# First 160 edge tiles as one dense matrix in both graph convolutions

## What is computed

```python
def _gcn(x, W, b, src, dst, w, n):
    h = x @ W
    agg = segment_sum(w[:, None] * h[src], dst, num_segments=n)
    return agg + b

f1 = layernorm(x)                              # 6250 x 256
h  = _gcn(f1, W1, b1, ...)                     # first convolution
z  = leaky(concat([h, root row of f1]))
z  = leaky(_gcn(z, W2, b2, ...))               # second convolution
x  = x + leaky(concat([z, root row of h]) @ Wl + bl)
n  = layernorm(x)
weights = n @ wr + br                          # router: the 3124 rows with the largest weights are chosen
x  = x + n + (chosen rows: (gelu(n @ w1 + b1) @ w2 + b2) * weight)
```

## Time and profile before

| | us |
|---|---|
| time, median of 3 runs | 2068.99 (2068.99 to 2077.73) |
| span of the profiled execution | 2915.3 |
| PE busy in it | 1865.9 |
| DVE busy | 1169.0 |
| GpSimd busy | 1474.9 |
| ACT busy | 369.1 |
| mean granted share of TensorE's full clock | 0.808 |

### The profile page before, as it was taken

One profiled execution on the slowest core, in us unless ns is written; L12 is line 12 of the kernel. 1 busy time (PEld: TensorE's weight loads), 2 busy tenths in 40 slices (PEclk: granted clock), 3 DMA queues, 4 the chain that ended last, 5 costly groups with the idle time before them and its releaser, 6 DMA issues.

```text
span 2915.3 us, 49425 instructions
## 1 busy us (share of the span) xinstructions
PE 1865.9 (64%) x7011; PEld 1437.8 (49%) x7012; DVE 1169.0 (40%) x4136; ACT 369.1 (13%) x927; POOL 1474.9 (51%) x1571
## 2 busy tenths in 40 slices
PE   0465646655555556354637888886777686757687
PEld 0344535434443444333526666665666465645475
DVE  6543333332332332222324455444544434434356
ACT  4200000000000000000101111111111111111111
POOL 5455555554555554455344555555555554545430
PEclk9788778777776776767878889988988888978797
DMA  6422222222222322222432222222222222222212
GB/s 202 131 83 81 80 80 80 84 78 74 82 81 78 88 79 75 70 79 77 152 98 72 72 72 81 78 79 75 78 81 76 81 71 69 83 62 82 67 50 88
DMA packets 120873, 244.27 MB, mean 84 GB/s; under 512 B 32822, under 2 KB 71046, under 8 KB 120748
## 3 DMA queue, kind: packets, MB, share of 16 engines
q0 software_dynamic: 73664, 200.90, 24.0%
q1 hardware_dynamic: 35612, 32.02, 3.5%
q10 hardware_dynamic: 11472, 10.27, 1.1%
HBM read 223.42 MB, written 19.64 MB: 83 GB/s over the span
## 4 chain that ended last, share of the span: by engine, by line
SPq 53%; issue 35%; PE 5%; DVE 3%; DVEq 1%; another core or an unknown queue 1%; DMA 1%; ACT 1%; ACTq 0%
SPq L348 45%; SPq L343 7%; PE ps_agg L716 2%; PE ps_dn L854 1%; PE ps_up L865 1%; DVE fw2s L1062 1%; DVE S L1153 0%; ACT xs L480 0%; DVE ring L1442 0%; DMA normed_rows<-xs 0%; DVEq L1193 0%; PE ps_o L804 0%; DVE acc L1161 0%; PE ps_dn L852 0%
## 5 line engine op out<-in xcount | busy, mean ns | idle before, releaser
L716 PE MATMUL ps_agg<-ring,S 128*128 x3136 | 912.1, 440 | 677.0 <-SPq L355 320.3
L716 PEld LDWEIGHTS ps_agg<-ring,S 128*128 128x128 f32 x3136 | 669.1, 221 | 860.1 <-issue 757.8
L434 POOL DMA_INDIRECT ring<-conv_rows,idx x752 | 714.5, 950 | 632.4 <-DVEq L1188 424.2
L434 POOL DMA_INDIRECT ring<-normed_rows,idx x736 | 701.1, 953 | 631.7 <-DVEq L1188 426.7
L1153 DVE TENSOR_SCALAR S<-iota,dstc,wc 128x128 f32<-128x128 int16 x1584 | 454.9, 353 | 377.1 <-issue 360.3
L1161 DVE TENSOR_TENSOR acc<-acc,ps_agg x490 | 206.3, 421 | 893.4 <-PE ps_agg L716 478.4
L716 PE MATMUL ps_agg<-ring,S_more 128*128 x768 | 265.7, 506 | 254.6 <-DVE S_more L1153 150.0
L716 PEld LDWEIGHTS ps_agg<-ring,S_more 128*128 128x128 f32 x768 | 187.6, 254 | 321.3 <-issue 287.9
L854 PE MATMUL ps_dn<-fw2s,hT 128*128 128x256 f32 x848 | 232.7, 434 | 0.0
L854 PEld LDWEIGHTS ps_dn<-fw2s,hT 128*128 128x128 f32 x848 | 179.4, 218 | 49.5 <-issue 21.7
L865 PE MATMUL ps_up<-xnT,fw1s 128*128 128x256 f32 x800 | 195.0, 400 | 8.9 <-issue 7.1
(11 more groups left out here) (248 smaller groups left out, 1077.2 us busy)
## 6 DMA issues: line engine op xcount, KB each, us to landing
ring<-normed_rows SPq DMA_DIRECT2D x2048, 1.0 KB
ring<-conv_rows SPq DMA_DIRECT2D x2048, 1.0 KB
ring<-conv_rows,idx POOLq DMA_INDIRECT x752
ring<-normed_rows,idx POOLq DMA_INDIRECT x736
conv_rows<-rows ACTq DMA_DIRECT2D x49, 128.0 KB
xs<-in_x SPq DMA_DIRECT2D x6, 640.0 KB
out_rows<-xs SPq DMA_DIRECT2D x3, 1024.0 KB
xs<-in_x SPq DMA_DIRECT2D x2, 1280.0 KB
```

Of the source, the lines that this page charges most:

```text
L434: pool.indirect_dma_start(out=ring[:, slot * TG + t, :], out_offset=None, in_=rows_of, in_offset=bass.IndirectOffsetOnAxis(ap=at, axis=0)) ...
L716: last = nc.tensor.matmul(to, select[:, t, :], moving, start=(t == 0), stop=(t == TG - 1))
```

## The change

The first 160 tiles (`NM`), which hold all edges whose destination is in windows 0 and 1, are taken out of the rounds. They become one matrix A with 256 columns (the destinations) and 50 blocks of 128 rows (the source nodes), held in SBUF in the place of `xs`. A round now has 12 tiles (`QG = 3`), the ring holds six groups, and there are 52 rounds (`NIT = NW + 3`). Steps start in round `lag`, which is now at least 4. With these inputs it comes out as 6, so 46 rounds have a step and two steps are left for after the last round.

Building A takes rounds 1 to 40 of the first convolution, four tiles a round. For each tile DVE writes a one-hot matrix of `src mod 128` (128 columns) and one of a key that joins `dst` within 5 nodes and the source block (245 columns, times the weight), PE multiplies them, and DVE adds the 49x5 result into A at a column read from a table. Rounds 41 to 50 multiply A by the rows in 10 chunks of 5 blocks and add 128x512 to windows 0 and 1. A is also stored to HBM. In the second convolution each round starts with one block of A (128x256, loaded by SyncE with its block of `conv_rows`), two matmuls into one half of `ps_agg` and one add of 128x512. SyncE's single-row copies and their tables are gone, so GpSimd gathers all other tiles: 622 per convolution, 22 of them from the raw input.

A branch for inputs in which one of the first 160 tiles spans more than 5 nodes (`rare_edges`) is there too; here the widest spans 5 nodes, so it is not taken.

The core of the diff:

```diff
-    QG = 4
+    QG = 3
+    NIT = NW + 3
+    NM = NT - NIT * RING
+    MW = 2
+    SPAN = 5
+    KEYS = SPAN * NW
+    BPER = 4
+    B_IT = 1 + NM // BPER
+    CHUNK = 5
@@ sync
-                    for i in range(FAR_PASS):
-                        p = c * FAR_PASS + i
-                        sp.dma_start(ring[p:p + 1, SLOTS * TG + b, :].bitcast(i8), rows_of[ds(offsets[i], D * 4)].unsqueeze(0)).then_inc(far_landed[l][b], 16)
+            def load_block(i):
+                a = max(0, NW - 1 - i)
+                m = a + 1 if i < NW else 0
+                sp.dma_start(block_a, a_dram[:, m, :]).then_inc(block_loaded, 16)
+                sp.wait_ge(t2_stored, 16 * (NW - a + 2))
+                sp.dma_start(block_t, t2_dram[a * P:(a + 1) * P, :]).then_inc(block_loaded, 16)
...
+            for i in range(1, NIT):
+                sp.wait_ge(block_used, i)
+                load_block(i)
@@ tensor
+            def build_tiles(it):
+                pe.wait_ge(build_added, it * BPER + 1)
+                pe.wait_ge(build_ready, it)
+                for t in range(BPER):
+                    last = nc.tensor.matmul(up_banks[:, t // 2, t % 2 * KEYS:(t % 2 + 1) * KEYS], src_hot[:, t, :], key_hot[:, t, :], start=True, stop=True)
+                last.then_inc(build_done, 1)
...
+            def dense_block(it):
...
+                pe.wait_ge(block_loaded, it * 32 + 32)
+                pe.wait_ge(acc_step[1], i + 1)
+                for m in range(MW):
+                    to = flat(ps_agg[:, ds(i & 1, 1), m * D:(m + 1) * D])
+                    last = nc.tensor.matmul(to, block_a[:, m * P:(m + 1) * P], block_t, start=True, stop=True)
+                last.then_inc(mm_done[1], 1)
+            def edge_round(l, it, steps, s=None, matrix_work=True):
+                if l == 1:
+                    dense_block(it)
+                for q in range(QG):
+                    edge_group(l, it, q)
+                    if l == 0 and q == 1 and matrix_work:
+                        first_nodes(it)
+                    for piece in steps[q] if steps else ():
+                        piece(s)
-            rounds(1, (turn_step1, ffn_step_a, conv_step1, ffn_step_b), NW - 1, late_weights_in)
+            rounds(1, ((turn_step1,), (ffn_step_a,), (conv_step1, ffn_step_b)), NW - 1, late_weights_in)
@@ vector
+            def add_block(i):
+                dve.wait_ge(mm_done[1], i + 1)
+                dve.wait_ge(acc_step[1], i + 1)
+                dve.sem_inc(block_used, 1)
+                V.tensor_tensor(first_acc, first_acc, flat(ps_agg[:, ds((i + 1) & 1, 1), :]), op=ALU.add).then_inc(acc_step[1], 1)
+            def hot_tiles(it):
+                for t in range(BPER):
+                    at = within(dve.snap(it * BPER + (t - BPER)), NM - 1)
+                    V.tensor_scalar(src_hot[:, t, :], iota[:, 0:P], src_low[:, ds(at, 1)], None, ALU.is_equal)
+                    last = V.tensor_scalar(key_hot[:, t, :], iota[:, 0:KEYS], keys[:, ds(at, 1)], wc[:, ds(at, 1)], ALU.is_equal, ALU.mult)
+                last.then_inc(build_ready, 1)
+            def add_tiles(it):
...
+                    base = within(dve.value_load(base_row[0:1, ds(at, 1)]), MSPAN - SPAN)
+                    to = matrix[:, :, ds(base, SPAN)]
...
+                    dve.wait_ge(build_added, it * BPER + (t + 1))
+                    of = up_banks[:, t // 2, t % 2 * KEYS:(t % 2 + 1) * KEYS].rearrange("p (r a) -> p a r", a=NW)
+                    V.tensor_tensor(to, to, of, op=ALU.add).then_inc(build_added, 1)
@@ edge_round of vector
-                    select_ahead(l, it, q)
...
+                    if l == 1 and q == 0:
+                        add_last(l, p0 - 1)
...
                     dve.sem_inc(group_used[l], 1)
+                    select_ahead(l, it, q)
+                    if l == 1 and q == 0:
+                        add_block(p0)
...
-            rounds(1, (x1_step, norm_step, no_step, no_step), NW - 1, last_norm)
+            rounds(1, (x1_step, norm_step, no_step), NW - 1, last_norm, lambda: dve.wait_ge(x_again, 16 * (len(XCH) + len(PART))))
```

More of the change, by code:

```diff
@@ L352, in far_done @@
[L352 to L368 removed]
+            sp.dma_start(*big_loads[2]).then_inc(last_layer_loaded, 16)
@@ L513, in rounds @@
                 with act.Fori(0, stop) as s:
-                    for q in range(QG):
-                        steps[q](s)
+                    for piece in steps:
+                        piece(s)
             def stage_sums(l, s):
@@ new lines, in dense_chunk @@
+            def dense_chunk(it):
+                half = within(pe.snap((it + B_IT) & 1), 1)
+                to = up_banks[:, ds(half, 1), :].rearrange("p b n -> p (b n)")
+                f0 = within(pe.snap(half * CHUNK), CHUNK)
+                pe.wait_ge(chunk_copied, it + 1)
+                pe.wait_ge(dense_added, it + 1)
+                pe.wait_ge(chunk_loaded[0], ((it + 1) >> 1) * 16 + 1)
+                pe.wait_ge(chunk_loaded[1], (it >> 1) * 16 + 1)
+                for m in range(MW):
+                    for k in range(CHUNK):
+                        row = within(pe.snap(f0 + k), 2 * CHUNK - 1) if k else f0
+                        last = nc.tensor.matmul(to[:, m * D:(m + 1) * D], chunk_a[:, k, m * P:(m + 1) * P], flat(blocks[:, ds(row, 1), :]), start=(k == 0), stop=(k == CHUNK - 1))
+                last.then_inc(dense_done, 1)
@@ L748, in rounds @@
+            def rounds(l, steps, stop, ahead_of_steps):
                 pe.reg_mov(extras, 0)
                 pe.reg_mov(step, 0)
-                d = within(pe.snap(first), NIT, 1)
-                with pe.Fori(0, d) as it:
-                    for q in range(QG):
-                        edge_group(l, it, q)
-                if ahead_of_steps is not None:
-                    ahead_of_steps()
+                d = within(pe.snap(first), NIT, NIT - NW + 1)
+                if l == 0:
+                    with pe.Fori(0, 1) as it:
+                        edge_round(l, it, None, None, False)
+                with pe.Fori(1 - l, d) as it:
+                    edge_round(l, it, None)
+                ahead_of_steps()
@@ L765, in rounds @@
                     with pe.Fori(done, stop) as s:
-                        for q in range(QG):
-                            steps[q](s)
-            def no_step(s):
-                pass
+                        for group in steps:
+                            for piece in group:
+                                piece(s)
             def first_root_term():
@@ L1244, in rounds @@
                         dve.reg_mov(step, s + 1)
-                end = within(dve.snap(within(dve.snap(extras), NG * NW) + NG), NG * (NW + 1))
+                with dve.Else():
+                    rare_edges(l)
+                end = within(dve.snap(within(dve.snap(extras), NG * NW) + NIT * PER[l]), MOST)
                 done = within(dve.snap(step), NIT - 1)
```

424 lines of the change are left out of this document (257 added, 167 removed).

## The result

The changed kernel takes **42,130.26 us** (median of 4, 42,117 to 42,139), the kernel before 2071.48 (2069 to 2078): **20.33 times** as long, interval 20.29 to 20.37. The forecast was 2130, range 1995 to 2215. The direction was right and the size was not: the case that I had given "under 0.01", the other branch, is what runs. So `lag` comes out as 52 and not as 6, and the branch that stands under The change as "not taken" is taken.

What follows compares the result with a forecast made beforehand. GpSimd's gathers bound the old kernel; after the change DVE would bound most of convolution 1 and a closed ring of waits convolution 2. 1000 + 92 + 948 + 22 + 74 = 2136, less 7: 2130 us, range 1995 to 2215.

Steps and rivals of the forecast that it cites:

- the case that I had given "under 0.01": A tile exceeds the allowed span, so `rare_edges` runs 7840 small products per convolution, tens of milliseconds; chance under 0.01.

Runs made afterwards that it cites:

- the one with 136 tiles: Changed kernel with A taking 136 tiles instead of 160, 54 rounds, span limit one higher: 2173.4 us (1.048); on the other kind of chip 2508.4 (0.862).

## What to carry to other kernels

Where a kernel has a fast path behind a test on its data, work the test out on the inputs with the kernel's own clamps and limits, at the last element first, before any round is summed: a branch that costs twenty times the whole outweighs every other term. When a product is moved to the head of a round, look for what stands ahead of it on its engine and whether that waits for the same round: here the same product ahead of the last two pieces of the step instead of behind them, together with `S_more` ahead of the next `S` on DVE, turned 4.8% slower into 6.3% faster, and where the two were tried apart the product had 112 of 141 us. And compare only with a run of the kernel before on the same chip, for a profile can come from a chip on which another engine sets the time.

## What the runs showed of the hardware

- The same program had two times by the chip: 2069 to 2072 us and 2909 to 2919 for the kernel before, 2173 and 2508 for the one with 136 tiles. The adds on DVE took 420 and 421 ns on both; but on the slower kind some register instructions took 0.7 us, or 1.4, where the median was 45 or 65 ns (on DVE 401 over 0.5 us against 9), and the kernel with 4096 small copies on SyncE lost most (41% against 15%).
- Profiling cost next to nothing: 2907.6 us profiled beside 2906 to 2929, and 2161.8 beside 2155 to 2160.
- PE waiting 1.24 us, then working 1.22, over and over, stayed at a granted clock of 0.50 for the whole of 19.8 ms; after 3.74 us of idle time in a round at full clock the next 4 products (8 records) took 3.77 us where they take 1.89, and the `down` behind them was slowed as well. With 0.85 us of idle time in the same place the product took 1.99.
